# Epsilon as a third triple of the statistics, and the reciprocal deviation as a repeated second tensor

## The chip, the cores and the metric

One Trainium2 chip, one core of it. The metric is device time in microseconds (us) of that core, median of the runs shown. The engines by their names in the profile: PE is TensorE (matrix products and transposes), PEld its weight loads, DVE is VectorE, ACT is ScalarE, POOL is GpSimd, SP is SyncE, which here only issues DMAs.

## The reference

A small language-model tower over 16 x 128 tokens with a width of 256: an embedding with its own normalisation, then four residual layers, each behind a layer normalisation.

```python
h = layernorm(word[ids] + pos[p] + type[t], eps=1e-12) * gamma + beta     # "E"
h = h + random_feature_attention(_layernorm(h))      # "P": q, k features exp(..), context, relu
h = h + prototype_experts_top2(_layernorm(h))        # "F": distances, two gates, rank-16 maps
h = h + causal_attention_with_rope(_layernorm(h))    # "R": 16 heads
h = h + ternary_mlp(_layernorm(h))                   # "M": 256 -> 1024 -> 256

def _layernorm(x, axis=-1, eps=1e-05):
    m = jnp.mean(x, axis=axis, keepdims=True)
    v = jnp.var(x, axis=axis, keepdims=True)
    return (x - m) / jnp.sqrt(v + eps)
```

Every token is independent except in the two attentions, which look at the 128 tokens of one sequence.

## The kernel before, in words

One tile is one sequence: 128 tokens on the 128 partitions, 256 features along the free dimension, in float32. There are 16 tiles. The residual rows of all tiles stay in SBUF (`hres`, `h_of(t)` is the row block of tile t).

The work of a tile is cut into about a hundred named operations ("Rst", "Rag", "Rrs", "Rxn", "Rtr", ...), each fixed to one engine. `ORDER` lists, engine by engine, the order in which that engine issues them; the n-th appearance of a name is its n-th tile. So some four or five tiles are in flight at different layers, and each engine works through its list strictly in order: an operation that has to wait holds up all that stands behind it on that engine. Engines wait for each other by semaphores (`wait(engine, sem, count)`).

A normalisation x (x is one of E, P, F, R, M) runs through these steps:

- `xst` (DVE): `bn_stats` over the 256 features of a token gives six numbers: count, mean and sum of squared deviations, once for the even and once for the odd features. These are two triples.
- `xag` (DVE): `bn_aggr` turns the triples into mean and variance, `mv[x]`. Behind it a `tensor_scalar` on one column adds the epsilon and writes `rstd[x][:, 0:1]` (lines 884, 893, 967, 1035, 1101). The residual is kept scaled by 256, so the epsilon is `RES_EPS = 256 * 256 * 1e-5` there and `EMB_EPS = 1e-12` for E.
- `xrs` (POOL): raises that to the power -0.5 with a `tensor_tensor` (lines 636, 652, 670, 685, 702), and for E, P and M forms minus mean times reciprocal deviation (`nmean`).
- the row scaling. For E, P and M it is ACT's activation with that scale and bias (`normalise`, line 1158). For F and R it is DVE's `tensor_scalar` with two per-partition scalars read from SBUF, mean and reciprocal deviation: `Fxn` (line 972) and `Rxn` (line 1039).
- PE transposes the scaled rows of F and R (`Ftr` line 1695, `Rtr` line 1805), ACT and DVE take the result to `xT` as two float16 parts, and the products follow.

POOL's list puts `Rrs` and `Frs` among long operations of its own: `qel` (line 666, 128x704), `rot` (692), `rl` (695), `hgl` (681), `esc`, `eh`, `e2`, `bb` and the low parts `Plo`, `onl`, `rol`, `Mlo`.

The start: DVE clears some constants (lines 1123 to 1126), waits for the token indices, which SP loads, clamps them (1129 to 1134), and POOL's gathers follow.

Of the kernel before, what the change touches and what calls it, by code (L numbers as in the profile page):

```python
# [16 lines left out]
P = 128  # L17
D = 256
# [210 lines left out]
def program(nc, A, out):  # L229
    with ExitStack() as ctx:  # L230
# [83 lines left out]
        def h_of(t):  # L314
            return hres[:, t, :]
# [107 lines left out]
        rows_zero = sem("rows_zero"); ge_set = sem("ge_set"); proj_zero = sem("proj_zero"); proj_in = sem("proj_in")  # L423
# [158 lines left out]
        def _(g):  # L582
# [16 lines left out]
            def step(op, t):  # L599
# [33 lines left out]
                elif op == "Ers":  # L633
                    wait(g, ag_ok["E"], 3 * t + 3)
                    wait(g, xn_ok["E"], t)
                    g.tensor_tensor(rstd["E"][:, 1:2], rstd["E"][:, 0:1], consts[:, :], ALU.pow).then_inc(rs_ok["E"], 1)
                    g.wait_ge(rs_ok["E"], t + 1)
                    g.tensor_scalar(nmean["E"][:, :], mv["E"][:, 0:1], rstd["E"][:, 1:2], -1.0, ALU.mult, ALU.mult)\  # L638
# [10 lines left out]
                elif op == "Prs":  # L649
                    wait(g, ag_ok["P"], 3 * t + 3)  # L650
                    wait(g, xn_ok["P"], t)
                    g.tensor_tensor(rstd["P"][:, 1:2], rstd["P"][:, 0:1], consts[:, :], ALU.pow).then_inc(rs_ok["P"], 1)
                    g.wait_ge(rs_ok["P"], t + 1)
                    g.tensor_scalar(nmean["P"][:, :], mv["P"][:, 0:1], rstd["P"][:, 1:2], -1.0, ALU.mult, ALU.mult)\
                        .then_inc(nm_ok["P"], 1)
                elif op == "Plo":
                    wait(g, hi_ok["P"], t + 1)
                    g.tensor_tensor(xs["P"][:, D:], xn["P"][:, :], xs["P"][:, 0:D], ALU.subtract).then_inc(lo_ok["P"], 1)
                elif op == "onl":
                    wait(g, hi_ok["o"], t + 1)  # L660
                    g.tensor_tensor(xs["o"][:, D:], onorm[:, :], xs["o"][:, 0:D], ALU.subtract).then_inc(lo_ok["o"], 1)
                elif op == "qel":
                    wait(g, qe1_ok, t + 1)
                    wait(g, qe2_ok, t + 1)
                    wait(g, qp_ok, 16 * t)
                    g.tensor_tensor(of_pairs(qel), in_pairs(qef), of_pairs(qeh), ALU.subtract).then_inc(qel_ok, 1)  # L666
                elif op == "Frs":
                    wait(g, ag_ok["F"], 3 * t + 3)
                    wait(g, xn_ok["F"], t)
                    g.tensor_tensor(rstd["F"][:, 1:2], rstd["F"][:, 0:1], consts[:, :], ALU.pow).then_inc(rs_ok["F"], 1)  # L670
                elif op == "dist":
                    wait(g, near_ok, t + 1)
                    wait(g, gap_ok, t)
                    g.tensor_tensor(dist[:, :], near[:, :], halves[:, :], ALU.pow).then_inc(dist_ok, 1)
                elif op == "gsl":
                    wait(g, gsh_ok, t + 1)
                    o = 2 * R2
                    g.tensor_tensor(hgs[:, o + PROTO:o + 2 * PROTO], gates[:, :], hgs[:, o:o + PROTO], ALU.subtract).then_inc(gsl_ok, 1)
                elif op == "hgl":
                    wait(g, hgh_ok, t + 1)  # L680
                    g.tensor_tensor(hgs[:, R2:2 * R2], hg[:, :], hgs[:, 0:R2], ALU.subtract).then_inc(hgl_ok, 1)  # L681
                elif op == "Rrs":
                    wait(g, ag_ok["R"], 3 * t + 3)
                    wait(g, xn_ok["R"], t)
                    g.tensor_tensor(rstd["R"][:, 1:2], rstd["R"][:, 0:1], consts[:, :], ALU.pow).then_inc(rs_ok["R"], 1)  # L685
                elif op == "rot":
                    wait(g, rope_ok, 3 * t + 3)
                    wait(g, rh1_ok, t)
                    wait(g, rh2_ok, t)
                    wait(g, rh3_ok, t)  # L690
                    wait(g, rl_ok, t)
                    g.tensor_tensor(rot[:, :, :].rearrange("p h d -> p (h d)"), rc[:, :], rs[:, :], ALU.add).then_inc(rot_ok, 1)  # L692
                elif op == "rl":
                    wait(g, rh1_ok, t + 1)
                    g.tensor_tensor(slots(32), rot[:, :, :], slots(16), ALU.subtract).then_inc(rl_ok, 1)  # L695
                elif op == "rol":
                    wait(g, hi_ok["r"], t + 1)
                    g.tensor_tensor(xs["r"][:, D:], rout[:, :], xs["r"][:, 0:D], ALU.subtract).then_inc(lo_ok["r"], 1)
                elif op == "Mrs":
                    wait(g, ag_ok["M"], 3 * t + 3)  # L700
                    wait(g, xn_ok["M"], t)
                    g.tensor_tensor(rstd["M"][:, 1:2], rstd["M"][:, 0:1], consts[:, :], ALU.pow).then_inc(rs_ok["M"], 1)
                    g.wait_ge(rs_ok["M"], t + 1)
                    g.tensor_scalar(nmean["M"][:, :], mv["M"][:, 0:1], rstd["M"][:, 1:2], -1.0, ALU.mult, ALU.mult)\
# [25 lines left out]
        def _(v):  # L730
# [142 lines left out]
            def step(op, t):  # L873
                if op in ONCE["DVE"]:
                    set_up(op)
                elif op == "Est":
                    wait(v, e2_ok, t + 1)
                    v.bn_stats(stats["E"][:, :], esum[:, :]).then_inc(ag_ok["E"], 1)
                elif op == "Eag":
                    wait(v, ag_ok["E"], 3 * t + 1)  # L880
                    wait(v, nm_ok["E"], t)
                    v.bn_aggr(mv["E"][:, :], stats["E"][:, :]).then_inc(ag_ok["E"], 1)
                    wait(v, ag_ok["E"], 3 * t + 2)
                    v.tensor_scalar(rstd["E"][:, 0:1], mv["E"][:, 1:2], EMB_EPS, None, ALU.add).then_inc(ag_ok["E"], 1)
                elif op == "Pst":
                    wait(v, eh_ok, t + 1)
                    v.bn_stats(stats["P"][:, :], h_of(t)).then_inc(ag_ok["P"], 1)
                elif op == "Pag":
                    wait(v, ag_ok["P"], 3 * t + 1)
                    wait(v, nm_ok["P"], t)  # L890
                    v.bn_aggr(mv["P"][:, :], stats["P"][:, :]).then_inc(ag_ok["P"], 1)
                    wait(v, ag_ok["P"], 3 * t + 2)
                    v.tensor_scalar(rstd["P"][:, 0:1], mv["P"][:, 1:2], RES_EPS, None, ALU.add).then_inc(ag_ok["P"], 1)
# [65 lines left out]
                elif op == "Fst":  # L959
                    wait(v, hP_ok, t + 1)  # L960
                    v.bn_stats(stats["F"][:, :], h_of(t)).then_inc(ag_ok["F"], 1)
                elif op == "Fag":
                    wait(v, ag_ok["F"], 3 * t + 1)
                    wait(v, xn_ok["F"], t)
                    v.bn_aggr(mv["F"][:, :], stats["F"][:, :]).then_inc(ag_ok["F"], 1)
                    wait(v, ag_ok["F"], 3 * t + 2)
                    v.tensor_scalar(rstd["F"][:, 0:1], mv["F"][:, 1:2], RES_EPS, None, ALU.add).then_inc(ag_ok["F"], 1)
                elif op == "Fxn":
# [3 lines left out]
                    v.tensor_scalar(xn["F"][:, :], h_of(t), mv["F"][:, 0:1], rstd["F"][:, 1:2], ALU.subtract, ALU.mult).then_inc(xn_ok["F"], 1)  # L972
# [54 lines left out]
                elif op == "Rst":  # L1027
                    wait(v, hF_ok, t + 1)
                    v.bn_stats(stats["R"][:, :], h_of(t)).then_inc(ag_ok["R"], 1)
                elif op == "Rag":  # L1030
                    wait(v, ag_ok["R"], 3 * t + 1)
                    wait(v, xn_ok["R"], t)
                    v.bn_aggr(mv["R"][:, :], stats["R"][:, :]).then_inc(ag_ok["R"], 1)
                    wait(v, ag_ok["R"], 3 * t + 2)
                    v.tensor_scalar(rstd["R"][:, 0:1], mv["R"][:, 1:2], RES_EPS, None, ALU.add).then_inc(ag_ok["R"], 1)  # L1035
                elif op == "Rxn":
                    wait(v, rs_ok["R"], t + 1)
                    wait(v, tr_ok["R"], t)
                    v.tensor_scalar(xn["R"][:, :], h_of(t), mv["R"][:, 0:1], rstd["R"][:, 1:2], ALU.subtract, ALU.mult).then_inc(xn_ok["R"], 1)  # L1039
# [53 lines left out]
                elif op == "Mst":  # L1093
                    wait(v, hR_ok, t + 1)
                    v.bn_stats(stats["M"][:, :], h_of(t)).then_inc(ag_ok["M"], 1)
                elif op == "Mag":
                    wait(v, ag_ok["M"], 3 * t + 1)
                    wait(v, nm_ok["M"], t)
                    v.bn_aggr(mv["M"][:, :], stats["M"][:, :]).then_inc(ag_ok["M"], 1)
                    wait(v, ag_ok["M"], 3 * t + 2)  # L1100
                    v.tensor_scalar(rstd["M"][:, 0:1], mv["M"][:, 1:2], RES_EPS, None, ALU.add).then_inc(ag_ok["M"], 1)
# [24 lines left out]
            v.memset(split[:, :], 0.0).then_inc(v_const, 1)  # L1126
            v.wait_ge(v_const, 6)
# [12 lines left out]
            v.memset(rows_all[BR:, :], 0.0).then_inc(rows_zero, 1)  # L1140
# [12 lines left out]
        def _(a):  # L1153
# [3 lines left out]
            def normalise(dst, src, x):  # L1157
                a.activation(dst, src, ACT.Identity, bias=nmean[x][:, 0:1], scale=rstd[x][:, 1:2]).then_inc(xn_ok[x], 1)  # L1158
# [251 lines left out]
        def _(pe):  # L1410
# [88 lines left out]
            def step(op, t):  # L1499
# [26 lines left out]
                elif op == "qk":  # L1526
# [4 lines left out]
                    if t == 0:  # L1531
                        pe.wait_ge(v_set, max(made("DVE", "zp1"), made("DVE", "zp3")))
                        pe.wait_ge(rows_zero, 1)
# [545 lines left out]
```

## Time and profile before

| what | value |
|---|---|
| time, median of 3 runs | 469.33 us |
| the runs | 470.93, 469.33, 463.96 us |
| span of the profiled execution, first to last instruction | 470.3 us |
| busy: PE, DVE, POOL, ACT | 401.4, 366.7, 284.0, 257.9 us |
| mean granted TensorE clock | 0.956 |

The span is the time from the first to the last instruction of one execution, which was recorded by the profiler; no other time is given for that execution. It lies 0.9 us above the median and 0.6 us below the highest of the three runs. The busy time of an engine is the time in which at least one of its computing instructions runs; on DVE two neighbours that do not depend on each other overlap slightly.

### The profile page before, as it was taken

The numbers are of one execution on the slowest core, as the hardware profiler recorded it, in microseconds if no ns is written. First come the engines' busy times: TensorE is split into PE (matmuls) and PEld (weight loads), VectorE is DVE, ScalarE is ACT, GpSimd is POOL, SyncE is SP. The second block draws the span as 40 slices with busy tenths as digits, with TensorE's granted clock in tenths as the row PEclk, the third lists the DMA queues.
The fourth block names the chain that finished last, engine by engine and source line by source line (L and its number), as shares of the span: only waits on it lengthen the run. The fifth ranks groups of instructions, "written<-read, shape, count | busy, mean of one in ns | idle before, by whom it ended". The sixth has DMA issues, their size and how long they took to land.

```text
span 470.3 us, 13968 instructions
## 1 busy us (share of the span) xinstructions
PE 401.4 (85%) x5026; PEld 273.4 (58%) x5026; DVE 366.7 (78%) x969; ACT 257.9 (55%) x573; POOL 284.0 (60%) x399
## 2 busy tenths in 40 slices
PE   8988768868898888799979797989898979797885
PEld 3444344535565667475747475656666656565664
DVE  4478899977999786999979698687878887766552
ACT  1246474547576555577738374647474736373541
POOL 7778888967577667677867655454555335252120
PEclk9998999979999899999989898898989998999999
DMA  4797542346464648455866484583767664611001
GB/s 135 183 291 189 144 102 26 70 100 106 102 118 92 116 91 140 106 119 96 138 113 107 96 121 88 94 152 68 95 104 127 116 91 74 101 36 24 13 13 35
DMA packets 145843, 48.55 MB, mean 103 GB/s; under 512 B 137264, under 2 KB 143216, under 8 KB 145776
## 3 DMA queue, kind: packets, MB, share of 16 engines
q1 hardware_dynamic: 144144, 43.21, 49.2%
q0 software_dynamic: 1632, 4.46, 3.4%
q8 instruction: 41, 0.67, 0.6%
q14 instruction: 26, 0.21, 0.2%
HBM read 11.80 MB, written 2.36 MB: 30 GB/s over the span
## 4 chain that ended last, share of the span: by engine, by line
PE 32%; issue 20%; DVE 15%; POOL 14%; DMA 9%; SPq 5%; ACT 4%; another core or an unknown queue 1%; POOLq 0%; DVEq 0%; ACTq 0%
PE PS L1415 11%; PE PS L2004 4%; PE PS L1925 2%; PE PS L2022 2%; DMA qkT<-qs 2%; DMA rTm<-split 2%; POOL split L695 2%; DMA rT<-split 1%; PE PS L1767 1%; PE PS L1626 1%; DVE xnR L1039 1%; DMA emb_type<-in_type,ids 1%; POOL qe L666 1%; SPq L534 1%
## 5 line engine op out<-in xcount | busy, mean ns | idle before, releaser
L1075 DVE TENSOR_REDUCE split<-PS 128x16 f16<-128x2048 f32 x16 | 36.8, 2297 | 10.3 <-PE PS L1494 7.6
L692 POOL TENSOR_TENSOR stage_f<-stage_f 128x512 f32<-128x512 f32 x16 | 21.0, 1310 | 27.7 <-DVE stage_f L1056 10.9
L1155 ACT ACTIVATE xTR<-PS 128x256 f16<-128x256 f32 x16 | 6.1, 382 | 49.6 <-PE PS L1805 49.6
L2004 PE MATMUL PS<-xTM,w1q 128*128 128x128 f16 x512 | 31.4, 219 | 0.0
L2004 PEld LDWEIGHTS PS<-xTM,w1q 128*128 128x128 f16 x512 | 28.6, 98 | 3.6 <-issue 3.6
L685 POOL TENSOR_TENSOR rstdR<-rstdR,consts 128x1 f32<-128x1 f32 x16 | 8.8, 553 | 32.9 <-DVE rstdR L1035 32.9
L666 POOL TENSOR_TENSOR qe<-qef,qe 128x704 f16<-128x704 f32 x16 | 25.3, 1580 | 5.4 <-ACT qe L1264 2.3
L1767 PE MATMUL PS<-faT_hi,hgT 128*128 128x256 f16 x128 | 25.8, 289 | 2.4 <-DMA hgT<-hgs 2.4
L1415 PE MATMUL PS<-rwqk_hi,xTR 128*128 128x512 f16 x64 | 27.2, 470 | 0.3
L1438 PE MATMUL PS<-warm 128*128 128x512 f16 x98 | 24.3, 415 | 1.4 <-DVE warm L1125 1.4
L1415 PE MATMUL PS<-wqkT_hi,xTP 128*128 128x512 f16 x64 | 23.9, 416 | 1.0 <-DMA xTP<-xsP 0.6
L681 POOL TENSOR_TENSOR hgs<-hg,hgs 128x512 f16<-128x512 f32 x16 | 19.5, 1220 | 7.2 <-ACT hgs L1155 7.0
L695 POOL TENSOR_TENSOR split<-stage_f,split 128x512 f16<-128x512 f32 x16 | 19.2, 1202 | 6.7 <-ACT split L1155 6.5
L1155 ACT ACTIVATE split<-stage_f 128x256 f16<-128x256 f32 (+1 forms) x48 | 21.8, 479 | 2.6 <-POOL stage_f L692 2.4
L1626 PEld LDWEIGHTS PS<-va,kp 128*88 128x88 f32 x256 | 21.9, 158 | 1.7 <-issue 0.8
L1626 PE MATMUL PS<-va,kp 128*88 128x34 f32 x256 | 22.2, 242 | 0.2 <-issue 0.2
L1415 PE MATMUL PS<-fbT_hi,xTF 128*128 128x512 f16 x64 | 21.7, 380 | 0.0
L1366 ACT ACTIVATE stage_p<-PS 128x1024 f32<-128x1024 f32 x16 | 16.4, 1025 | 8.4 <-PE PS L1494 8.4
L1158 ACT ACTIVATE ehat<-esum,nmeanE,rstdE 128x256 f32<-128x256 f32 x16 | 9.5, 593 | 21.0 <-POOL nmeanE L638 21.0
L1427 PE MATMUL PS<-proj_hi,qkT 64*128 64x88 f16 x256 | 14.8, 208 | 5.8 <-DMA qkT<-qs 3.6
L907 DVE TENSOR_REDUCE PS<-PS 128x16 f32<-128x704 f32 x16 | 14.3, 895 | 6.7 <-PE PS L1427 6.5
L1438 PEld LDWEIGHTS PS<-warm 128*128 128x128 f16 x98 | 10.2, 105 | 14.9 <-issue 3.9
(328 smaller groups left out, 1426.0 us busy)
## 6 DMA issues: line engine op xcount, KB each, us to landing
out<-outb SPq DMA_DIRECT2D x16, 128.0 KB, 2.0
w<-in_w1T SPq DMA_DIRECT2D x1, 1024.0 KB
w<-in_w2T SPq DMA_DIRECT2D x1, 1024.0 KB
stage_p<-in_wqkT SPq DMA_DIRECT2D x1, 512.0 KB, 4.6
stage_f<-in_fbT SPq DMA_DIRECT2D x1, 512.0 KB
stage_f<-in_faT SPq DMA_DIRECT2D x1, 512.0 KB
stage_r<-in_rwqk SPq DMA_DIRECT2D x1, 512.0 KB, 6.0
rT<-split SPq DMA_TRANSPOSE x26, 3.6
```

What stands on the lines that cost most here:

```text
L666: g.tensor_tensor(of_pairs(qel), in_pairs(qef), of_pairs(qeh), ALU.subtract).then_inc(qel_ok, 1)
L681: g.tensor_tensor(hgs[:, R2:2 * R2], hg[:, :], hgs[:, 0:R2], ALU.subtract).then_inc(hgl_ok, 1)
L692: g.tensor_tensor(rot[:, :, :].rearrange("p h d -> p (h d)"), rc[:, :], rs[:, :], ALU.add).then_inc(rot_ok, 1)
L695: g.tensor_tensor(slots(32), rot[:, :, :], slots(16), ALU.subtract).then_inc(rl_ok, 1)
L1075: v.tensor_reduce(slots(SLOT - DH)[:, 0:H, DH - 1].rearrange("p (c j) -> p j c", j=4), PS[:, BANK["s1"]:BANK["s1"] + 4, :].rearrange("p j ...
L1155: return a.activation(dst, src, ACT.Copy)
L1366: a.activation(pfull[:, 2:4, :, :], PS[:, BANK["s1"] + 2:BANK["s1"] + 4, :].rearrange("p j (c q) -> p j c q", c=4), ACT.Exp)\
L1415: last = pe.matmul(dst, xT[x][:, xp, :], wp[:, c, :], start=(n == 0), stop=(n == 3 * KC - 1 and bias is None))
L1438: last = pe.matmul(PS[:, SET_BANK, :], warm[:, 0:P], warm[:, :], start=(j == 0), stop=(j == n - 1))
L1626: last = pe.matmul(PS[0:MP, BANK["ctx"], 2 * VA * j:2 * VA * (j + 1)], kp[:, (j % 2 * 4 + j // 2) * MP:(j % 2 * 4 + j // 2 + 1) * MP], va[ ...
L1767: pe.matmul(PS[:, BANK["y"], 0:D], hgT[:, xp, :], wp[:, c, :], start=(c == 0 and xp == 0 and wp is whi["faT"]), stop=False)
L2004: last = pe.matmul(PS[:, BANK["m1"] + f // 4, f % 4 * P:(f % 4 + 1) * P], w1q[:, n % KC, f * P:(f + 1) * P], xT["M"][:, n, :], start=False ...
```

## The change

It does two things.

The epsilon moves into the aggregation. `stats[x]` becomes a view of nine numbers, the two triples that `bn_stats` writes and a third one that is set once at the start: count 0, mean 0, sum of squares 256 times the epsilon. `bn_aggr` takes all nine, and the variance that it gives already holds the epsilon. The one-column `tensor_scalar` behind it is gone, and POOL takes the power of `mv[x][:, 1:2]`. The counts of the `ag_ok` semaphores go from three to two per tile, and `xst` also waits for the `xag` of the tile before. Three small memsets are added at DVE's start.

The two row scalings of DVE become `scalar_tensor_tensor`: the mean is still a per-partition scalar, and the reciprocal deviation is now the second tensor, one column read 256 times (`bc` is `to_broadcast`). `ORDER` is the same on every engine.

```diff
-        stats = {x: sb(f"stats{x}", [P, 6]) for x in LNS}
+        triples = sb("triples", [P, len(LNS), 9])
+        stats = {x: triples[:, n, :] for n, x in enumerate(LNS)}
...
-        rstd = {x: sb(f"rstd{x}", [P, 2]) for x in LNS}
+        rstd = {x: sb(f"rstd{x}", [P, 1]) for x in LNS}
...
                 elif op == "Rrs":
-                    wait(g, ag_ok["R"], 3 * t + 3)
+                    wait(g, ag_ok["R"], 2 * t + 2)
                     wait(g, xn_ok["R"], t)
-                    g.tensor_tensor(rstd["R"][:, 1:2], rstd["R"][:, 0:1], consts[:, :], ALU.pow).then_inc(rs_ok["R"], 1)
+                    g.tensor_tensor(rstd["R"][:, :], mv["R"][:, 1:2], consts[:, :], ALU.pow).then_inc(rs_ok["R"], 1)
...
                 elif op == "Rst":
                     wait(v, hF_ok, t + 1)
-                    v.bn_stats(stats["R"][:, :], h_of(t)).then_inc(ag_ok["R"], 1)
+                    wait(v, ag_ok["R"], 2 * t)
+                    v.bn_stats(stats["R"][:, 0:6], h_of(t)).then_inc(ag_ok["R"], 1)
                 elif op == "Rag":
-                    wait(v, ag_ok["R"], 3 * t + 1)
+                    wait(v, ag_ok["R"], 2 * t + 1)
                     wait(v, xn_ok["R"], t)
-                    v.bn_aggr(mv["R"][:, :], stats["R"][:, :]).then_inc(ag_ok["R"], 1)
-                    wait(v, ag_ok["R"], 3 * t + 2)
-                    v.tensor_scalar(rstd["R"][:, 0:1], mv["R"][:, 1:2], RES_EPS, None, ALU.add).then_inc(ag_ok["R"], 1)
+                    v.bn_aggr(mv["R"][:, :], stats["R"]).then_inc(ag_ok["R"], 1)
                 elif op == "Rxn":
                     wait(v, rs_ok["R"], t + 1)
                     wait(v, tr_ok["R"], t)
-                    v.tensor_scalar(xn["R"][:, :], h_of(t), mv["R"][:, 0:1], rstd["R"][:, 1:2], ALU.subtract, ALU.mult).then_inc(xn_ok["R"], 1)
+                    v.scalar_tensor_tensor(out=xn["R"][:, :], in0=h_of(t), scalar=mv["R"][:, 0:1], in1=bc(rstd["R"][:, :], [P, D]),
+                                           op0=ALU.subtract, op1=ALU.mult).then_inc(xn_ok["R"], 1)
...
             v.memset(split[:, :], 0.0).then_inc(v_const, 1)
+            v.memset(triples[:, :, 6:8], 0.0).then_inc(rows_set, 1)
+            v.memset(triples[:, 0:1, 8:9], D * EMB_EPS).then_inc(rows_set, 1)
+            v.memset(triples[:, 1:, 8:9], D * RES_EPS).then_inc(rows_set, 1)
```

The same edits stand for E, P, F and M; only F and R have a row scaling on DVE. The first `Est` and the first `qk` wait until the constants are set.

## Rows read from the trace of the kernel before

**Rows 1.** the head and the busy times of the page, and its chain that ended last, by engine

```profile
span 470.3 us, 13968 instructions
PE 401.4 (85%) x5026; PEld 273.4 (58%) x5026; DVE 366.7 (78%) x969; ACT 257.9 (55%) x573; POOL 284.0 (60%) x399
...
PE 32%; issue 20%; DVE 15%; POOL 14%; DMA 9%; SPq 5%; ACT 4%; another core or an unknown queue 1%; POOLq 0%; DVEq 0%; ACTq 0%
```

**Rows 2.** busy time of each engine in the stretch from 100 to 400 us

```profile
core 0: us, PE busy (x) PEld busy (x) DVE busy (x) ACT busy (x) POOL busy (x), PEclk, DMA share, GB/s
100.00:400.00 300.00, 265.59 (x3580) 187.05 (x3581) 249.81 (x664) 182.69 (x418) 183.79 (x262) 0.94 0.61 107
```

**Rows 3.** VectorE's groups by line and shape (xcount, busy us, mean ns, idle before)

```profile
L1039 DVE TENSOR_SCALAR xnR<-hres,mvR,rstdR 128x256 f32<-128x256 f32 x16 | 12.1, 754 | 1.1 <-POOL rstdR L685 1.1
...
L972 DVE TENSOR_SCALAR xnF<-hres,mvF,rstdF 128x256 f32<-128x256 f32 x16 | 11.3, 705 | 1.2 <-POOL rstdF L670 1.1
...
L1025 DVE SCALAR_TENSOR_TENSOR hres<-PS,wsum,hres 128x256 f32<-128x256 f32 x16 | 7.7, 479 | 4.3 <-PE PS L1769 4.3
...
L957 DVE SCALAR_TENSOR_TENSOR hres<-PS,hres 128x256 f32<-128x256 f32 x16 | 6.6, 414 | 0.6 <-PE PS L1419 0.3 <-issue 0.3
...
L1033 DVE BATCH_NORM_AGGREGATE mvR<-statsR 128x2 f32<-128x6 f32 x16 | 2.8, 177 | 0.4
...
L1035 DVE TENSOR_SCALAR rstdR<-mvR 128x1 f32<-128x1 f32 x16 | 2.5, 154 | 0.6
```

**Rows 4.** timeline of one aggregation of the fourth normalisation (start, duration, us)

```profile
212.73 0.18 DVE L1033 BATCH_NORM_AGGREGATE mvR<-statsR 128x2 f32<-128x6 f32 x1
...
212.94 0.15 DVE L1035 TENSOR_SCALAR rstdR<-mvR 128x1 f32<-128x1 f32 x1
...
213.01 0.42 DVE L878 BATCH_NORM_STATS2 statsE<-esum 128x6 f32<-128x256 f32 x1
...
213.18 0.55 POOL L685 TENSOR_TENSOR rstdR<-rstdR,consts 128x1 f32<-128x1 f32 x1 [0.20 <-DVE rstdR L1035]
```

**Rows 5.** the two row scalings, durations ns minimum, median, maximum

```profile
L1039 DVE TENSOR_SCALAR xnR<-hres,mvR,rstdR x16: 397/803/1606, 75.9 to 427.1; 128x256 f32<-128x256 f32 x16
...
L972 DVE TENSOR_SCALAR xnF<-hres,mvF,rstdF x16: 396/522/1595, 56.9 to 410.4; 128x256 f32<-128x256 f32 x16
```

**Rows 6.** timeline of a row scaling that meets a GpSimd operation

```profile
264.50 0.66 POOL L708 TENSOR_TENSOR xsM<-xnM,xsM 128x256 f16<-128x256 f32 x1
...
264.57 0.74 DVE L1039 TENSOR_SCALAR xnR<-hres,mvR,rstdR 128x256 f32<-128x256 f32 x1
```

**Rows 7.** timeline of two scalar_tensor_tensor of the set-up, beside GpSimd's operations

```profile
59.30 0.79 POOL L632 TENSOR_TENSOR esum<-hres,emb 128x256 f32<-128x256 f32 x1
...
59.53 0.84 DVE L762 SCALAR_TENSOR_TENSOR fb<-fbias,fb_hi 64x256 f16<-64x256 f32 x1
...
76.99 1.26 DVE L870 SCALAR_TENSOR_TENSOR w1q<-w,thr,wneg 128x1024 f16<-128x1024 f32 x1
...
77.17 2.47 POOL L666 TENSOR_TENSOR qe<-qef,qe 128x704 f16<-128x704 f32 x1 [0.48 <-ACT qe L1264]
```

**Rows 8.** GpSimd's group of the operation that such a row met (columns as above)

```profile
L666 POOL TENSOR_TENSOR qe<-qef,qe 128x704 f16<-128x704 f32 x16 | 25.3, 1580 | 5.4 <-ACT qe L1264 2.3 <-issue 2.1 <-ACT qef L1260 0.9
```

**Rows 9.** pieces of the chain that ended last (start, us, what)

```profile
14.05 0.16 DVE rstdE L884
...
56.85 0.03 DVE xnF L972
...
337.51 0.03 DVE rstdR L1035
...
427.07 0.82 DVE xnR L1039
```

**Rows 10.** the waits of PE, in total (us, times, longest us)

```profile
PE PS L1805 <- DVE xnR L1039: 9.4, 11, 1.6
```

**Rows 11.** timeline of VectorE at the start, the first operation on the indices

```profile
2.64 0.24 DVE L1129 SCALAR_TENSOR_TENSOR ids_neg<-ids,id_count 128x48 int32<-128x48 int32 x1 [0.19 <-DMA ids<-in_ids]
```

More of the change, by code:

```diff
@@ L633, in step @@
                 elif op == "Ers":
-                    wait(g, ag_ok["E"], 3 * t + 3)
+                    wait(g, ag_ok["E"], 2 * t + 2)
                     wait(g, xn_ok["E"], t)
-                    g.tensor_tensor(rstd["E"][:, 1:2], rstd["E"][:, 0:1], consts[:, :], ALU.pow).then_inc(rs_ok["E"], 1)
+                    g.tensor_tensor(rstd["E"][:, :], mv["E"][:, 1:2], consts[:, :], ALU.pow).then_inc(rs_ok["E"], 1)
                     g.wait_ge(rs_ok["E"], t + 1)
-                    g.tensor_scalar(nmean["E"][:, :], mv["E"][:, 0:1], rstd["E"][:, 1:2], -1.0, ALU.mult, ALU.mult)\
+                    g.tensor_scalar(nmean["E"][:, :], mv["E"][:, 0:1], rstd["E"][:, 0:1], -1.0, ALU.mult, ALU.mult)\
                         .then_inc(nm_ok["E"], 1)
@@ L649, in step @@
                 elif op == "Prs":
-                    wait(g, ag_ok["P"], 3 * t + 3)
+                    wait(g, ag_ok["P"], 2 * t + 2)
                     wait(g, xn_ok["P"], t)
-                    g.tensor_tensor(rstd["P"][:, 1:2], rstd["P"][:, 0:1], consts[:, :], ALU.pow).then_inc(rs_ok["P"], 1)
+                    g.tensor_tensor(rstd["P"][:, :], mv["P"][:, 1:2], consts[:, :], ALU.pow).then_inc(rs_ok["P"], 1)
                     g.wait_ge(rs_ok["P"], t + 1)
-                    g.tensor_scalar(nmean["P"][:, :], mv["P"][:, 0:1], rstd["P"][:, 1:2], -1.0, ALU.mult, ALU.mult)\
+                    g.tensor_scalar(nmean["P"][:, :], mv["P"][:, 0:1], rstd["P"][:, 0:1], -1.0, ALU.mult, ALU.mult)\
                         .then_inc(nm_ok["P"], 1)
@@ L960, in step @@
                     wait(v, hP_ok, t + 1)
-                    v.bn_stats(stats["F"][:, :], h_of(t)).then_inc(ag_ok["F"], 1)
+                    wait(v, ag_ok["F"], 2 * t)
+                    v.bn_stats(stats["F"][:, 0:6], h_of(t)).then_inc(ag_ok["F"], 1)
                 elif op == "Fag":
-                    wait(v, ag_ok["F"], 3 * t + 1)
+                    wait(v, ag_ok["F"], 2 * t + 1)
                     wait(v, xn_ok["F"], t)
-                    v.bn_aggr(mv["F"][:, :], stats["F"][:, :]).then_inc(ag_ok["F"], 1)
-                    wait(v, ag_ok["F"], 3 * t + 2)
-                    v.tensor_scalar(rstd["F"][:, 0:1], mv["F"][:, 1:2], RES_EPS, None, ALU.add).then_inc(ag_ok["F"], 1)
+                    v.bn_aggr(mv["F"][:, :], stats["F"]).then_inc(ag_ok["F"], 1)
                 elif op == "Fxn":
@@ L971, in step @@
                     wait(v, xsq_ok, t)
-                    v.tensor_scalar(xn["F"][:, :], h_of(t), mv["F"][:, 0:1], rstd["F"][:, 1:2], ALU.subtract, ALU.mult).then_inc(xn_ok["F"], 1)
+                    v.scalar_tensor_tensor(out=xn["F"][:, :], in0=h_of(t), scalar=mv["F"][:, 0:1], in1=bc(rstd["F"][:, :], [P, D]),
+                                           op0=ALU.subtract, op1=ALU.mult).then_inc(xn_ok["F"], 1)
                 elif op == "FT":
@@ L1094, in step @@
                     wait(v, hR_ok, t + 1)
-                    v.bn_stats(stats["M"][:, :], h_of(t)).then_inc(ag_ok["M"], 1)
+                    wait(v, ag_ok["M"], 2 * t)
+                    v.bn_stats(stats["M"][:, 0:6], h_of(t)).then_inc(ag_ok["M"], 1)
                 elif op == "Mag":
-                    wait(v, ag_ok["M"], 3 * t + 1)
+                    wait(v, ag_ok["M"], 2 * t + 1)
                     wait(v, nm_ok["M"], t)
-                    v.bn_aggr(mv["M"][:, :], stats["M"][:, :]).then_inc(ag_ok["M"], 1)
-                    wait(v, ag_ok["M"], 3 * t + 2)
-                    v.tensor_scalar(rstd["M"][:, 0:1], mv["M"][:, 1:2], RES_EPS, None, ALU.add).then_inc(ag_ok["M"], 1)
+                    v.bn_aggr(mv["M"][:, :], stats["M"]).then_inc(ag_ok["M"], 1)
                 elif op == "MV":
```

38 lines of the change are left out of this document (19 added, 19 removed).

## The prediction

> **What bounds the kernel now.** I read the head of the page first: PE is busy for 401.4 us of a span of 470.3, DVE for 366.7, POOL for 284.0 [rows 1]. No engine is full. In the long middle (100 to 400 us) the picture is the same: of 300 us PE has 265.6, DVE 249.8, POOL 183.8 [rows 2]. The reader is to see two engines at 89% and 83%, each of which goes through a fixed list, so that each waits for the other by turns. That is why the second view is the chain of work that ended last: PE holds 32% of it, "issue" 20%, DVE 15%, POOL 14%, DMA 9% [rows 1]. It passes from engine to engine again and again; DVE's time is worth its full length only where the chain runs on DVE. The third view is PE's waits: it stands still 11 times, 9.4 us together, for the row scaling of R [rows 10]. So this change touches the path, at the fourth normalisation above all. The times of DVE's operations come from its groups [rows 3] and from stretches of the timeline.
>
> **The epsilon's own instruction goes (80 times).** There are 5 in each of 16 tiles, 154 ns each [rows 3]. They cost less than that, since neighbours overlap. In the timeline the aggregation starts at 212.73, the addition at 212.94, the next independent operation at 213.01 [rows 4]: 0.28 us from aggregation to next. Without the addition the next one starts where it may overlap the aggregation's end by the same 0.08 us as it now overlaps the addition's (212.94 + 0.15 - 213.01), so 0.18 - 0.08 = 0.10 us behind it. Saved: 0.18 us here; over many such places I read 0.19 as typical. 80 x 0.19 = 15.2 us of DVE. POOL's power, which waits for the result (213.18, [rows 4]), can start 0.18 us earlier too, as the addition's start-to-end chain (212.94 - 212.73 + 0.15 = 0.36) shrinks to the aggregation's 0.18.
>
> **How much of that lies on the path.** I counted the pieces of the chain that are one of the five additions: 16 of 80 (7 of R, 4 of E, 3 of P, 2 of F, none of M), the first at 14.05, the last at 337.51 [rows 9]. 16 x 0.19 = 3.0 us. Within this reading that is also a ceiling: shortening an operation shortens the longest path by no more than its share in it, and other paths keep their length.
>
> **The aggregation of nine numbers for six.** No row shows it. The nearest: the aggregation of six takes 177 ns, a one-column operation 154 [rows 3]. From below it costs nothing; from above it grows with its input, 9/6 x 177 = 266, +89 ns (7.1 us of DVE, 16 x 0.089 = 1.4 us on the chain). It can't be a gain, since it does more. I take the slope between the two rows, 23 ns for five numbers, so +14 ns for three: 1.1 us of DVE, 0.2 us on the chain.
>
> **The row scalings (32 times).** Before, they last 754 and 705 ns on average [rows 3], but 397 and 396 at least, 1606 and 1595 at most [rows 5]. Looking through them one by one: 10 of R's 16 and 8 of F's 16 are above 0.45 us, the other 14 lie at 0.40 to 0.415. All the long ones but one overlap a POOL arithmetic operation that had begun before or with them, and end right behind it (one meets a gather). In [rows 6] POOL's low part runs 264.50 to 265.16 and the scaling ends at 265.31: 0.15 us behind. The excess, (754 - 397) x 16 + (705 - 397) x 16, is 10.6 us, 0.59 each on the 18. So DVE is locked out while POOL works. The question is whether the new form is locked out too. The set-up answers it: a `scalar_tensor_tensor` with both tensors in SBUF, 256 columns, starts at 59.53 beside POOL's addition that ends at 60.09 and takes 0.84 us, to 60.37, 0.28 us behind POOL's end; in the other order an operation of that kind holds from 76.99 to 78.25 while POOL's begins at 77.17 and lasts 2.47 us [rows 7] against a mean of 1.58 for its group [rows 8]. So the new form waits as the old does, and behind the lock it ends 0.28 us later instead of 0.15: +0.13. Free, the nearest row is the same operation with one pointer scalar (from PSUM), 479 ns, against 414 for one without a pointer [rows 3] and 397 for the old form: +0.08. Sum on DVE: 18 x 0.13 + 14 x 0.08 = 3.5 us. On the chain are 14 scalings (9 of R, 5 of F, from 56.85 to 427.07, [rows 9]), 10 locked and 4 free: 1.3 + 0.3 = 1.6 us. The bounds: 0.02 us each (414 against 397, a pointer at no cost: 0.3 us on the chain) and 0.28 each if a locked one restarted in full (479 - 0.15 - 0.05: 3.9 us on the chain).
>
> The rows say +0.08 free and +0.13 locked. The Trainium skill (VectorE: DVE Perf Modes, The perf-mode tier table) has float32 `tensor_scalar` in SBUF at twice the rate of a two-tensor operation, which for 256 columns at its 0.96 GHz makes an estimate of +0.13 us for every one: 14 x 0.13 = 1.8 us on the chain in place of 1.6. The trace agrees for the locked ones; for the free ones it shows less, since the old form's two pointers cost it part of its lead. The skill also says (SBUF — State Buffer, Who interferes with whom) that a DVE instruction with two SBUF inputs contends with a GpSimd instruction that reads SBUF, and this speaks against any relief from the lock; by that rule, the 0.84 us of [rows 7] agrees.
>
> **Small things.** The three memsets come before DVE's wait for the indices, where it idles 0.19 us [rows 11]; its memsets of that size start 0.03 us apart there, so some 0.1 us is hidden, and 0.2 would be the cost without the cover. The added wait of `xst` on the aggregation of the tile before is met a whole tile earlier; behind it on DVE stands what stood there. `xag` already has two waits, and DVE idles 0.4 us in 16 before it [rows 3], no more than a single wait costs. POOL's lines change only their operands. The queues of SP and POOL are passed by nothing.
>
> **Sum.** DVE: -15.2 + 1.1 + 3.5 = -10.6 us of work. The path: -3.0 + 0.2 + 1.6 = -1.2 us. 470.3 - 1.2 = 469.1 for an execution like the profiled one, whose span lies 1.0 above the median of 469.3: 468.1, say 468.0 us. What is late next behind a shorter DVE stretch is mostly POOL (the power, 0.55 us, [rows 4], stays) and PE.
>
> **Rivals.**
>
> A, more locks lost (slower). `Rxn` and `Fxn` are released by POOL's power, behind which POOL takes its next operation at once. Who comes first gets the memory. Today DVE often still works at something else at that moment; with 0.19 us less in front of it, it stands ready more often, just behind POOL's start. Each of the 14 free ones that becomes locked costs on average 0.59 + 0.05 us, and 14 of 32 scalings are on the chain, so 0.28 us of path each. From about four more (1.2 / 0.28) the kernel is slower than before; if all 14 lose, +3.9 us, and the sum is 470.3 + 2.7 - 1.0 = 472.0. For it: the lock is decided by hundredths of a microsecond [rows 6]. Against: the same shift also frees some.
>
> B, the new form isn't locked out. Then the 10 locked scalings on the chain lose 0.59 each, 5.9 us, and all 14 last 0.48: +1.1. With the additions: -5.9 + 1.1 - 3.0 = -7.8, 470.3 - 7.8 - 1.0 = 461.5 us. For it: the repeated column needs little reading. Against: [rows 7], two tensors in SBUF waited.
>
> C, DVE's work counts in full, because DVE at 83% is the true limit of the middle and the chain only one of many equal ones: -10.6, 470.3 - 10.6 - 1.0 = 458.7. Against: its 17% idle and the ceiling above.
>
> D, the change doesn't bring the lighter aggregation: nine numbers cost +89 ns. -3.0 + 1.4 + 1.6 = 0: 469.3 us.
>
> **How the numbers follow.** Chances: the forecast 0.62 (between 465 and 470.5), A 0.14, B 0.10, C 0.06, D 0.08. The three runs before spread over 7 us, so I don't make the edges sharper than that: 460.5 to 472 takes in the forecast, B, D and most of A, and leaves out C and the outer half of A. A difference under 2% (9.4 us, so 459.9 to 478.7) is about what a measurement of this kernel can't tell from none. Faster by more: C and the lower edge of B, 0.08. Slower by more: only if the lock and the order of arrivals work against it well beyond A, 0.02. Within: 0.90.
>
> **What the profile after would show.** The five one-column groups gone; the aggregation at about 190 ns (D: 260); the two scalings at least 476 ns, with a mean near 0.85 us and again about half of them ending 0.28 us behind a POOL operation (B: all at 0.48; A: more than 18 above 0.55); DVE's busy time near 356; PE's wait for `Rxn` about 9 us still. I am wrong if the lock goes or doubles, if the granted clock differs between the two, or if the chain is a poor measure and the saved 0.19 us per normalisation passes through five times a tile.

## The result, and the profile after

The changed kernel took 473.53 us (median of 4 runs, 468.91 to 474.04) against 468.26 us for the kernel before (4 runs, 463.96 to 470.93): ratio 1.0121, 95% interval 1.0066 to 1.0177. It was forecast to gain 0.3% and came out slower. Two later comparisons with more runs gave 1.0030 (0.9978 to 1.0083) and 1.0059 (1.0020 to 1.0098). Weighted by their intervals the three make 1.0066 (1.0039 to 1.0093): a loss of 0.4 to 0.9%, some 3 us, and no gain, though the second comparison alone would allow one. The ratio leaves out runs more than 1.5% above the fastest of the same kernel, the medians do not. From one comparison to the next the median of the kernel before lies anywhere from 462.2 to 468.3 us, so only numbers of one comparison are set against each other.

The head of the page of the changed kernel, and its chain by engine, which answer to [rows 1]:

```profile
span 472.0 us, 13967 instructions
PE 398.3 (84%) x5026; PEld 272.7 (58%) x5026; DVE 358.4 (76%) x892; ACT 257.5 (55%) x573; POOL 286.3 (61%) x399
...
PE 31%; issue 20%; POOL 19%; DVE 12%; DMA 11%; ACT 5%; SPq 2%; another core or an unknown queue 0%; POOLq 0%; DVEq 0%; ACTq 0%
```

DVE did 8.3 us less than before, of 10.6 forecast, and the span didn't shorten. The same in the middle stretch, against [rows 2]:

```profile
100.00:400.00 300.00, 261.82 (x3579) 185.68 (x3579) 243.40 (x604) 181.54 (x418) 185.28 (x262) 0.96 0.60 106
```

DVE's groups of the changed kernel (mean ns behind the busy time), against [rows 3]:

```profile
L1039 DVE SCALAR_TENSOR_TENSOR xnR<-hres,mvR,rstdR 128x256 f32<-128x256 f32 x16 | 14.1, 882 | 1.2 <-POOL rstdR L686 1.0
...
L972 DVE SCALAR_TENSOR_TENSOR xnF<-hres,mvF,rstdF 128x256 f32<-128x256 f32 x16 | 11.3, 705 | 1.8 <-POOL rstdF L671 1.6
...
L1035 DVE BATCH_NORM_AGGREGATE mvR<-triples 128x2 f32<-128x9 f32 x16 | 3.1, 191 | 0.4
```

The aggregation of nine numbers takes 14 ns more, as forecast, and the one-column additions are gone. R's scaling grew from 754 to 882 ns. Its spread (minimum, median, maximum), against [rows 5]:

```profile
L1039 DVE SCALAR_TENSOR_TENSOR xnR<-hres,mvR,rstdR x16: 470/938/1737, 74.7 to 427.1; 128x256 f32<-128x256 f32 x16
```

```profile
L972 DVE SCALAR_TENSOR_TENSOR xnF<-hres,mvF,rstdF x16: 464/485/1728, 55.9 to 410.1; 128x256 f32<-128x256 f32 x16
```

A scaling that meets no operation of POOL takes 0.46 to 0.49 us (0.40 to 0.415 before). One that meets an arithmetic operation of POOL is locked out: it ends 0.28 us behind POOL's end, in all 17 cases, where the old form ended 0.15 us behind. The same scaling as in [rows 6], in the timeline of the changed kernel:

```profile
270.64 0.66 POOL L709 TENSOR_TENSOR xsM<-xnM,xsM 128x256 f16<-128x256 f32 x1
270.65 0.93 DVE L1039 SCALAR_TENSOR_TENSOR xnR<-hres,mvR,rstdR 128x256 f32<-128x256 f32 x1
```

POOL ends at 271.30, the scaling at 271.58. R has 11 locked scalings (10 before), F 6 (8 before).

The longer scaling holds POOL up as well. Of POOL's two additions that meet R's last scaling the second begins inside it; before and after:

```profile
427.00 1.45 POOL L621 TENSOR_TENSOR hres<-hres,b 128x256 f32<-128x256 f32 x2
```

```profile
427.05 1.59 POOL L622 TENSOR_TENSOR hres<-hres,b 128x256 f32<-128x256 f32 x2
```

Where this execution gives the gain back can be looked for at R. I took the mean over the 16 tiles from the start of the operation that ends layer F (line 1025 before, 1026 after) to the start of ACT's copy of R's transpose: 4.11 us before, 4.14 after. Up to the start of the scaling it is 2.41 us in place of 2.60, the 0.19 of the removed addition; the scaling takes 0.88 in place of 0.75; from its end to PE's transpose pass 0.28 in place of 0.17. PE's wait for it grew from 9.4 us [rows 10]:

```profile
PE PS L1808 <- DVE xnR L1039: 10.9, 12, 1.6
```

One profile of each kernel says less than it seems to. A second profile of the kernel before (the last run below) has 8 locked scalings of R instead of 10, 3.86 us from F's end to ACT's copy instead of 4.11, and a shorter wait of PE:

```profile
PE PS L1805 <- DVE xnR L1039: 6.1, 10, 1.1
```

The changed kernel's two further profiles have 11 locked scalings of R again, 4.19 and 4.11 us, and waits of 10.3 and 10.2 us. So the stretch is longer in the changed kernel by 0.0 to 0.3 us a tile, depending on which profiles are compared.

At the start of R's scaling, tile by tile, the changed kernel was ahead by 1.3 us at 97 us, behind by 6 us at 270, level at 409 and behind by 1.7 at the end. One step of almost 4 us, at 142, begins with a DMA: PE gets `hgT` late, the transposed expert activations of layer F. The first product on it, in this profile and in the third one of the changed kernel:

```profile
140.05 0.27 PE L1770 MATMUL PS<-faT_hi,hgT 128*128 128x256 f16 x1 [1.92 <-DMA hgT<-hgs]
```

```profile
139.24 0.27 PE L1770 MATMUL PS<-faT_hi,hgT 128*128 128x256 f16 x1 [1.90 <-DMA hgT<-hgs]
```

In the kernel before the same product started at 138.16, without a wait, though SP had issued its DMA 0.3 us later (135.13 against 134.83). Behind 140.5 the granted clock was at half (1.2 GHz) for 3.4 us in this one profile; the late DMA isn't peculiar to it. At this tile PE waits 1.6 to 1.9 us for `hgT` in all three profiles of the changed kernel, and not at all in the kernel before, its repeat, or the kernel with the new scalings alone. The transposing DMAs of `hgT` are slower throughout (minimum, median, maximum from issue to landing, before and after):

```profile
DMA to landing us min/median/max: 2.9/3.2/5.1
```

```profile
DMA to landing us min/median/max: 3.3/3.8/5.3
```

and PE's waits for them, before and after:

```profile
PE PS L1767 <- DMA hgT<-hgs: 2.4, 4, 1.5
```

```profile
PE PS L1770 <- DMA hgT<-hgs: 4.7, 6, 1.9
```

What the change also does, and the prediction didn't price, is move buffers. `triples` and the smaller `rstd` together take more of each partition, and all buffers allocated behind them lie 32 bytes later: in the built program `hgs` starts at byte 194304 of its partition before and at 194336 after. The times to landing of the 18 profiles part cleanly by this. In the nine without such a shift (the kernel before, its repeat, the new scalings alone, the doubled scalings, whose spare tiles shift by 2048 bytes, and the waits on GpSimd laid on these) the fastest `hgT` lands in 2.86 to 2.88 us and the median `rTm`, another transposing DMA, in 2.73. In the nine with a shift (32 bytes in all kernels with the epsilon in the aggregation, 160 in the one with the addition twice) they take 3.23 to 3.31 and 3.2. The shifted kernels include one with less work on DVE and one with more, so it isn't the work that parts them. PE's waits for `hgT` are 2.2 us on average in the first nine, 4.1 in the others, its waits for all DMAs 20.0 and 22.9, though single profiles overlap. So the shift may cost some 2 to 3 us; that is an estimate from these waits. No run moves the buffers alone, so that the address is the cause isn't shown.

### The profile page after: what moved, and what is told of

Its sections match the earlier page's. It is cut to its first block, busy times and chain, and to the rows that moved or that the text cites. A ratio compares the mean times of both kernels' runs of the same rounds, so it can differ in the third digit from the quotient of the medians.

```text
span 472.0 us, 13967 instructions
## 1 busy us (share of the span) xinstructions
PE 398.3 (84%) x5026; PEld 272.7 (58%) x5026; DVE 358.4 (76%) x892; ACT 257.5 (55%) x573; POOL 286.3 (61%) x399
## 4 chain that ended last, share of the span: by engine, by line
PE 31%; issue 20%; POOL 19%; DVE 12%; DMA 11%; ACT 5%; SPq 2%; another core or an unknown queue 0%; POOLq 0%; DVEq 0%; ACTq 0%
PE PS L1418 11%; PE PS L2007 5%; DMA rTm<-split 3%; PE PS L1928 2%; PE PS L2025 2%; POOL qe L667 2%; PE PS L1629 2%; DMA qkT<-qs 2%; POOL hgs L682 2%; POOL wneg L617 2%; DMA rT<-split 2%; DVE split L1076 1%; DMA row_qk<-in_bqk 1%; POOL split L696 1%; PE PS L1913 1%
## 5 line engine op out<-in xcount | busy, mean ns | idle before, releaser
L2007 PE MATMUL PS<-xTM,w1q 128*128 128x128 f16 x512 | 32.4, 223 | 0.0
L2007 PEld LDWEIGHTS PS<-xTM,w1q 128*128 128x128 f16 x512 | 29.7, 100 | 3.8 <-issue 3.8
L686 POOL TENSOR_TENSOR rstdR<-mvR,consts 128x1 f32<-128x1 f32 x16 | 8.9, 555 | 33.0 <-DVE mvR L1035 33.0
L1418 PE MATMUL PS<-rwqk_hi,xTR 128*128 128x512 f16 x64 | 25.5, 441 | 0.3
L1418 PE MATMUL PS<-wqkT_hi,xTP 128*128 128x512 f16 x64 | 22.6, 394 | 0.5 <-issue 0.5
L1418 PE MATMUL PS<-fbT_hi,xTF 128*128 128x512 f16 x64 | 22.7, 396 | 0.0
L1369 ACT ACTIVATE stage_p<-PS 128x1024 f32<-128x1024 f32 x16 | 16.4, 1025 | 8.3 <-PE PS L1497 8.3
L1430 PE MATMUL PS<-proj_hi,qkT 64*128 64x88 f16 x256 | 14.4, 204 | 6.9 <-DMA qkT<-qs 4.2
L597 POOL DMA_INDIRECT hres<-in_word,ids x16 | 17.1, 1072 | 3.2 <-issue 2.2
```

Source lines behind the costliest of these rows:

```text
L597: g.indirect_dma_start(dst, None, table, bass.IndirectOffsetOnAxis(rows_, 0)).then_inc(g_ok[slot], 16)
L1418: last = pe.matmul(dst, xT[x][:, xp, :], wp[:, c, :], start=(n == 0), stop=(n == 3 * KC - 1 and bias is None))
L2007: last = pe.matmul(PS[:, BANK["m1"] + f // 4, f % 4 * P:(f % 4 + 1) * P], w1q[:, n % KC, f * P:(f + 1) * P], xT["M"][:, n, :], start=False ...
```

## The experiments

### The two parts, each alone, and the change again

Theory 1: the longer row scaling costs the time, on the path of R. Theory 2: the shorter aggregation shifts the engines so that DMAs and locks fall worse. Epsilon alone, on the changed kernel (F likewise):

```diff
-                    v.scalar_tensor_tensor(out=xn["R"][:, :], in0=h_of(t), scalar=mv["R"][:, 0:1], in1=bc(rstd["R"][:, :], [P, D]),
-                                           op0=ALU.subtract, op1=ALU.mult).then_inc(xn_ok["R"], 1)
+                    v.tensor_scalar(xn["R"][:, :], h_of(t), mv["R"][:, 0:1], rstd["R"][:, 0:1], ALU.subtract, ALU.mult).then_inc(xn_ok["R"], 1)
```

> The epsilon inside the aggregation alone, both row scalings still the tensor_scalar with two per-partition scalars. Theory 1 (the new form of the row scaling costs the time: +0.13 us behind the lock, +0.08 us free, on the path of the fourth normalisation): this kernel is faster than before, ratio 0.990 to 0.998, since it only takes 0.19 us out 80 times. Theory 2 (the shorter aggregation shifts the engines against each other, so that DMAs and locks fall worse): it is slower by about as much as the changed kernel, ratio 1.005 to 1.015. Theory 3 (the two together, neither alone): within 0.995 to 1.003.

Measured: 460.78 us (12 runs) against 462.41 (29 runs), ratio 0.9963 (0.9919 to 1.0008). The mean from layer F's end to ACT's copy is 3.90 us, no less than in the repeat of the kernel before (3.86). Theory 2 expected a loss of 0.5% or more and falls. The edit gains 0.4% by the ratio, with an interval that just takes in no change, while DVE's busy time is 355.3 us, 9 to 11 less than in the two profiles of the kernel before (364.6 and 366.7). It carries the shift of 32 bytes with it: its fastest `hgT` lands in 3.26 us.

The scalings alone, on the kernel before (F likewise):

```diff
-                    v.tensor_scalar(xn["R"][:, :], h_of(t), mv["R"][:, 0:1], rstd["R"][:, 1:2], ALU.subtract, ALU.mult).then_inc(xn_ok["R"], 1)
+                    v.scalar_tensor_tensor(out=xn["R"][:, :], in0=h_of(t), scalar=mv["R"][:, 0:1], in1=bc(rstd["R"][:, 1:2], [P, D]),
+                                           op0=ALU.subtract, op1=ALU.mult).then_inc(xn_ok["R"], 1)
```

> The two row scalings in the new form alone, the one-column addition kept. Theory 1: slower than before by more than the changed kernel, since nothing is taken out: ratio 1.010 to 1.02, the scalings at 0.48 us free and 0.13 us longer than before when locked. Theory 2: about as before, ratio 0.998 to 1.005 (14 of 32 scalings on the chain, 1.6 us).

Measured: 464.59 us, ratio 1.0031 (0.9979 to 1.0083), R's scaling at 878 ns. In sign as theory 1 has it, in size below its range and inside that of theory 2; the interval takes in no change. The layout is that of the kernel before.

The changed kernel once more:

> The changed kernel once more, on this chip and beside the same runs of the kernel before, to see how large and how steady its loss is. Theories 1 and 2 both expect 1.005 to 1.017. A ratio under 1.003 would say that the first comparison was mostly the spread of runs.

Measured: 464.46 us, ratio 1.0030 (0.9978 to 1.0083). The first +1.2%, from four runs a side, lies mostly above what this one finds; the two intervals overlap.

### What time at these places is worth

The scaling twice, on the kernel before (F likewise):

```diff
+                    v.tensor_scalar(spare["R"][:, :], h_of(t), mv["R"][:, 0:1], rstd["R"][:, 1:2], ALU.subtract, ALU.mult)
                     v.tensor_scalar(xn["R"][:, :], h_of(t), mv["R"][:, 0:1], rstd["R"][:, 1:2], ALU.subtract, ALU.mult).then_inc(xn_ok["R"], 1)
```

> The kernel before with each of the 32 row scalings of VectorE issued twice, the first time into a spare tile that nobody reads (extra work that the reference doesn't ask for). It measures what a longer scaling at this place is worth: about +0.32 us each (0.40 less the overlap of 0.08), four times the +0.08 of the new form. Theory 1 (every piece of the fourth normalisation's scaling is paid once a tile, amplified): slower by 2% or more, ratio 1.015 to 1.03. Theory 2 (scalings count only by their share in the chain, 14 of 32 x 0.32 = 4.5 us): ratio 1.005 to 1.012.

Measured: 478.43 us, 16.0 above before's median, ratio 1.037 (1.031 to 1.043). DVE's busy time on its page is 381.1, 14.4 more than in [rows 1] (16.5 more than in the repeat): all of it is paid, and PE's waits show where most of it goes:

```profile
PE PS L1808 <- DVE xnR L1042: 17.6, 14, 2.6
...
PE PS L1698 <- DVE xnF L974: 5.0, 5, 1.5
```

9.4 us had become 17.6 for R [rows 10], and 2.0 had become 5.0 for F. The spare tiles move the buffers by a multiple of 256 bytes, and `hgT` lands as before (2.86 us at best). A count of the scalings on the chain, 14 of 32, forecast 1.2% at most and falls.

The addition twice, in all five normalisations, on the kernel before (half the epsilon each time):

```diff
-                    wait(v, ag_ok["R"], 3 * t + 2)
-                    v.tensor_scalar(rstd["R"][:, 0:1], mv["R"][:, 1:2], RES_EPS, None, ALU.add).then_inc(ag_ok["R"], 1)
+                    wait(v, ag_ok["R"], 4 * t + 2)
+                    v.tensor_scalar(half["R"][:, :], mv["R"][:, 1:2], 0.5 * RES_EPS, None, ALU.add).then_inc(ag_ok["R"], 1)
+                    wait(v, ag_ok["R"], 4 * t + 3)
+                    v.tensor_scalar(rstd["R"][:, 0:1], half["R"][:, :], 0.5 * RES_EPS, None, ALU.add).then_inc(ag_ok["R"], 1)
```

> The kernel before with the epsilon added in two halves, one behind the other, in all five normalisations: the one-column instruction whose removal is the first part of the change now stands there twice (80 more, each dependent on the one before, 0.19 us). It doubles what the change takes away. If time on VectorE passes through in full wherever it is (15 us): ratio 1.03. If only the pieces on the chain count (16 x 0.19 = 3.0 us): 1.005 to 1.009. If, as the kernel with the epsilon in the aggregation alone suggests (ratio 0.996), about a ninth to a quarter passes: 1.003 to 1.010.

Measured: 471.10 us (6 runs) against 462.53 (29), ratio 1.0264 (1.0177 to 1.0351). That is near the 1.03 expected if time on DVE passes through in full. DVE's busy time is 376.1, 9.4 us above [rows 1] and 11.6 above the repeat. So adding about 10 us costs 8 to 16, and taking about 10 away gained 0 to 4. It would be rash to read a law in that. Both kernels move the buffers (by 160 and by 32 bytes), and in both `hgT` lands late: 3.31 us at best here, and PE waits 6.8 us for it against 2.4. If the shift costs 2 to 3 us in each, it takes that from the gain and adds it to the loss, and the two come nearer to each other. No run separates the two.

### The lock

GpSimd waits behind its power until the scaling is done, on the kernel before (for F: the same with F's names, line 670):

```diff
                     g.tensor_tensor(rstd["R"][:, 1:2], rstd["R"][:, 0:1], consts[:, :], ALU.pow).then_inc(rs_ok["R"], 1)
+                    g.wait_ge(xn_ok["R"], t + 1)
```

> The kernel before, with one wait more on GpSimd: behind the power of the fourth normalisation (R) it waits until VectorE's row scaling of R is done, before it takes its next operation. That takes the lock away from 10 scalings of R, whose excess is 5.7 us in all (mean 0.75 against 0.40), and holds GpSimd up by 0.45 us or more, 16 times. Theory L (the time in which a row scaling is locked out is paid in full, as the doubled scalings were, 14.5 us of added work for 17 us): faster, ratio 0.985 to 0.993. Theory S (the lock only replaces another wait, since the pieces on the chain are few): 0.997 to 1.003. Slower if GpSimd's own operations (the low part of the exponentials above all, 1.5 us) are the path: 1.005 and more.

> The same for the third normalisation (F) alone: GpSimd waits behind F's power until VectorE's row scaling of F is done. 8 locked scalings, excess 4.9 us. More stands between aggregation and scaling on VectorE here, so GpSimd waits longer, up to 2 us. Theory L: 0.990 to 0.997 less what GpSimd loses. Theory S: 1.000 to 1.01.

Measured: R 459.69 us, ratio 1.0020 (0.9963 to 1.0076); F 461.44 us, ratio 1.0016 (0.9964 to 1.0068), before 462.53. No scaling is locked out where the wait stands; each alone can't be told from no change by the ratio; the medians lie 0.6% and 0.2% below that of the kernel before. That speaks for theory S and against L, as far as one wait alone goes. Both together, on the kernel before, in a later comparison:

> The kernel before with GpSimd's two waits alone (behind the power of R and of F). If the lock eats the epsilon's gain (theory E): this alone brings little, ratio 0.994 to 1.000, and the epsilon's edit on top of it (h4) 1% more. If the waits bring the whole gain (theory W): 0.984 to 0.989, and h4 lies within 0.3% of it.

Measured: 459.20 us (6 runs) against 467.72 (23), ratio 0.9849 (0.9785 to 0.9913). DVE's groups of this kernel:

```profile
L974 DVE TENSOR_SCALAR xnF<-hres,mvF,rstdF 128x256 f32<-128x256 f32 x16 | 6.5, 409 | 5.3 <-POOL rstdF L670 5.1
L1041 DVE TENSOR_SCALAR xnR<-hres,mvR,rstdR 128x256 f32<-128x256 f32 x16 | 6.5, 406 | 0.7 <-POOL rstdR L686 0.7
```

754 and 705 ns [rows 3] have become 406 and 409. The two waits together gain 1.5%, more than the parts let hope. They take 8 to 10 us of busy time off DVE (356.3) and gain 7 us by the ratio, 8.5 by the medians, although POOL now waits. So time taken out of the row scalings is paid for about as well as time put in.

With the epsilon in the aggregation on top, in three comparisons:

> The epsilon inside the aggregation, the row scalings as before the change, and both waits of GpSimd, behind the power of R and of F. If theory L holds and the parts add up: 0.996 x 0.989 x 0.994, about 0.98. If theory S holds: about 0.996 to 1.005.

Measured: 457.44 us, ratio 0.9953 (0.9902 to 1.0003), medians -1.1%: not the 0.98 of theory L.

> The epsilon in the aggregation, the old scalings, and GpSimd's two waits, once more: the version that the experiments point to. If its lead is real: median 4 to 6 us under the median of the kernel before, ratio 0.985 to 0.998. If it was spread: 0.998 to 1.004.

Measured: 454.85 us against 462.23, ratio 0.9849 (0.9802 to 0.9895).

> The epsilon in the aggregation, old scalings, GpSimd's two waits, beside h1 on the same chip. Theory E: 0.985, a full 1% below h1. Theory W: within 0.3% of h1.

Measured: 462.17 us against 467.72, ratio 0.9880 (0.9837 to 0.9923), no better than the two waits alone beside it (0.9849). Theory E, which wanted 1% more on top of the waits, falls; theory W's 0.3% is just met by the ratios, and the median is 3.0 us higher instead of lower. The lock doesn't hide a gain of the epsilon's edit; a gain above 0.5% is outside what the two intervals allow. The slower `hgT` is in this kernel too (3.23 us at best, 2.88 in the one with the two waits alone).

The changed kernel with the two waits:

> The changed kernel with GpSimd's two waits behind the power of R and F, so that no row scaling is locked out. If the new form costs 0.08 us free and nothing else, this lies 0.2 to 0.5% above the kernel with the epsilon in the aggregation, the old scalings and the same two waits: ratio 0.993 to 1.000, scalings at 0.48 us throughout. If the new form costs more than its own length (through what it keeps GpSimd from): 1.003 and more.

Measured: 455.95 us, ratio 0.9845 (0.9779 to 0.9910); both scalings at 0.48 us:

```profile
L1041 DVE SCALAR_TENSOR_TENSOR xnR<-hres,mvR,rstdR 128x256 f32<-128x256 f32 x16 | 7.6, 478 | 1.1 <-POOL rstdR L687 1.0
L974 DVE SCALAR_TENSOR_TENSOR xnF<-hres,mvF,rstdF 128x256 f32<-128x256 f32 x16 | 7.6, 477 | 5.2 <-POOL rstdF L671 5.1
```

Not locked out, the new form costs 1.1 us of median over the old one (454.85) and nothing by the ratio (0.9845 and 0.9849), all within the intervals.

The new form of the scalings and the two waits, on the kernel before:

> The same with the row scalings in the new form, the addition kept. The new form is 0.08 us longer when free, 32 times, 2.6 us at most. Both theories: 0 to 0.5% above h1.

Measured: 465.49 us, ratio 0.9952 (0.9906 to 0.9999): 1.0% above the two waits alone, more than the 0.5% expected, with intervals that just overlap. DVE's busy time is only 2.4 us longer.

The doubled scalings with the two waits:

> The row scalings issued twice (the first into a spare tile), with GpSimd's two waits: the added work is now 32 x 0.32 = 10 us, no lock. Without the waits the doubled scalings cost 3.7%. If that was mostly the lock met twice: ratio to h1 under 1.012. If a scaling's length is paid in full: 1.022 above h1.

Measured: 471.42 us, ratio 1.0110 (1.0031 to 1.0189), 12.2 us above the median of the two waits alone (2.6%, where 2.2% was expected if the length is paid) for 9.9 us more on DVE (366.2 against 356.3). PE's wait for R's scaling with the two waits alone, and here:

```profile
PE PS L1807 <- DVE xnR L1041: 5.9, 9, 1.2
```

```profile
PE PS L1810 <- DVE xnR L1044: 9.8, 13, 1.5
```

So the cost of the doubled scalings wasn't the lock met twice; a scaling's length itself is paid in full. POOL stands behind the scaling in this kernel and is held up with it; without the waits (478.43 us) it wasn't made to, and there the length was paid too.

### Two controls

The changed kernel a third time:

> The changed kernel a third time. Theory N (its parts nearly cancel: the epsilon's part is worth about -0.4%, the longer row scalings about +0.3 to +0.5%, and the first comparison's +1.2% from four runs a side was largely spread): ratio 0.998 to 1.006. Theory P (a real loss of 1% that the second comparison missed by chance): 1.008 to 1.015.

Measured: 463.05 us against 462.23, ratio 1.0059 (1.0020 to 1.0098).

The kernel before against itself:

> The kernel before under a name of its own, against itself: what this comparison makes of no change. Ratio 1.000 within its interval; a deviation of 0.3% or more would say that differences of that size are not to be read from one comparison.

Measured: 462.26 us, ratio 1.0014 (0.9977 to 1.0052). 1.0059 is inside theory N's range (the parts nearly cancel) at its upper end; theory P's 1% isn't reached. What is left is a small loss. Differences of 0.2% aren't to be read from one of these comparisons.

## Why the prediction was wrong

**Durations: right.** Aggregation +14 ns (forecast +14); scaling +0.08 us free and +0.13 locked (both as forecast); 17 locked scalings of 32 where there were 18. DVE -8.3 us against -10.6.

**The step that failed: "How much of that lies on the path", as it was used for the scalings.** The prediction priced them by how many stand on one recorded chain ("On the chain are 14 scalings"), 14 of 32, and put 1.6 us for them. The doubled scalings test this price: by the count they should have cost 4.5 us, they cost 16.0 for 14.4 us of DVE's busy time, and 12.2 for 9.9 with the lock taken away. A microsecond there costs about a microsecond, whether or not the chain ran through it in that execution. By the forecast's own durations that makes 18 x 0.13 + 14 x 0.08 = 3.5 us instead of 1.6; the groups of the first profile show 2.0 us more busy time. It isn't that PE waits for every scaling: it waits 11 times for R's and 3 times for F's before, 14 and 5 times when they are doubled. How the others pass their delay on isn't traced.

**The additions.** Their gain was put at 3.0 us by the same count. Measured were 1.7 (460.78 against 462.41, between a loss of 0.4 and a gain of 3.7), so the forecast lies inside the interval and this run doesn't refute it; beside the two waits nothing was gained. The argument that the share in the chain is a ceiling holds for a removal. The scalings grew, and for what grows the share in one chain is no ceiling, since another path can become the longest; they were priced by the same count all the same.

**A term that was put at nothing.** "Small things" has no line for the memory layout. The slower transposing DMAs go with it in every profile, and PE's waits put it at 2 to 3 us, by estimate. -1.2, with the scalings at 3.5 instead of 1.6 and 2 to 3 for the layout, makes about +3, which is what the three comparisons together show (+0.66%). That the sum fits doesn't show its terms: the layout wasn't tested by itself, and the scalings alone measured 1.0031 (0.9979 to 1.0083).

**Sum.** By ratio, -1.7 us for the epsilon alone (its layout included) and +1.4 us for the scalings alone make about 0; the changed kernel itself stood at +1.4 and +2.7 us by ratio (1.0030 and 1.0059 of 462), +5.7 in the first comparison. Forecast was -1.2. The upper end was too low as well: 473.53 lies 1.5 us above it. The range was built from three runs, whose spread of 7 us was known, and rival A's worst case closed it; later 29 runs of the kernel before lay between 457.66 and 467.80 us on one chip. Why the first comparison came out at 1.2%, above both others, stays open.

**Rivals.** A (more locks lost): no, 17 for 18. B (the new form isn't locked out): no, 1737 ns at most. C (DVE's work counts in full): not for the whole change, which took 8.3 us off DVE and lost time; for the row scalings nearly so, put in (1.037) or taken out (0.9849 with the two waits). D (dear aggregation): no, 191 ns.

**The page's rule** that a DVE instruction with two SBUF inputs contends with a GpSimd instruction that reads SBUF (the Trainium skill, SBUF — State Buffer, Who interferes with whom): the trace agrees, 11 of R's 16 new scalings waited for POOL's end.

**Still open:** how much of the epsilon's gain the moved buffers take back. The kernel before with 32 unused bytes ahead of `xnP` would show it, and so would the changed kernel padded to a shift of 256 bytes; no run has either. PE's wait for R's scaling doesn't decide it: 6.8 us in the profile of the epsilon alone, 6.1 in the repeat of the kernel before.

## What to carry to other kernels

Before a chain is used to price an edit, ask who waits for the operation, and test the price by issuing it twice; how often it stands on one recorded chain said 4.5 us where 16 were paid. When an edit changes the size of a buffer, compare the DMAs' times from issue to landing too, since everything allocated behind it has moved; a run that moves the buffers and does nothing else belongs beside it. Profile the unchanged kernel twice before a wait is compared: here PE's wait for one operation was 9.4 and 6.1 us in the same kernel. Where two engines share access to memory and a small operation of one releases the other, let the first wait until the other is through: here two waits of GpSimd gained 1.5%, more than any other edit alone.

## What the runs showed of the hardware

A `tensor_scalar` of 256 float32 columns with two per-partition scalars takes 0.40 us free and up to 1.6 us when it meets POOL's 1.5 us operation; the `scalar_tensor_tensor` with a repeated column as second tensor takes 0.48 and up to 1.74. The wait is for the whole of POOL's operation, though it began as little as 0.06 us before. POOL is held up in turn: an addition that begins inside a scaling takes 0.77 us beside the old form and 0.91 beside the new. Repeating one column instead of reading a full tensor gives no relief: both end 0.28 us behind POOL.

The transposing DMA of `hgT` lands in 2.86 to 2.88 us at best in nine profiles, and in 3.23 to 3.31 in nine whose buffers lie 32 or 160 bytes further; other transposes (`qkT`, 3.05 to 3.08 at best in all) don't change. That the address is the cause isn't shown beyond this parting.

The best versions measured are the kernel before with GpSimd's two waits (0.9849) and the same with the epsilon in the aggregation (0.9849, 0.9880 and 0.9953 in three comparisons); the changed kernel with the waits isn't told apart from them (0.9845).
